# Extra products of constants on TensorE in the half phases without expert blocks

## What is computed

```
x = x + attention(layernorm(x))      # 16 heads of 8; softmax row sums times v, then an output product
x = x + experts(layernorm(x))        # top 2 of 8 experts, 128 -> 512 -> relu -> 128
x = x + selective_scan(layernorm(x)) # 16 states, cumulative sums over tokens
x = x + experts(layernorm(x))        # the same experts again
```

## Time and profile before

| | us |
|---|---|
| median of three runs | 1569.88 (1565.36 to 1571.23) |
| the profiled execution | 1570.4 |
| its span, first to last instruction | 1568.7 |
| PE busy in it | 1017.3 (65%) |
| DVE busy | 827.3 (53%) |
| ACT busy | 743.9 (47%) |
| POOL busy | 629.0 (40%) |
| mean granted clock of TensorE | 0.77 of full speed |

### The profile page before, as it was taken

How to read it: one execution, slowest core, us unless ns; L and a number is a source line. 1 busy time by engine, 2 the same in 40 slices (tenths; PEclk the granted TensorE clock), 3 DMA queues, 4 the chain that set the end, 5 groups by cost and what they waited for, 6 DMA issues and landing times. The chain is left out here.

```text
span 1568.7 us, 18068 instructions
## 1 busy us (share of the span) xinstructions
PE 1017.3 (65%) x5080; PEld 752.7 (48%) x5080; DVE 827.3 (53%) x2789; ACT 743.9 (47%) x2034; POOL 629.0 (40%) x672
## 2 busy tenths in 40 slices
PE   4777689558887673687888643477686536772372
PEld 2554477426664432575576321356375215561272
DVE  4676555555666683556556645254555534545011
ACT  4786666546565662565556513153364232450020
POOL 2101200362424366423223466654444576465303
PEclk8665698678788575888879566788899768896696
DMA  8001244213230012333543111243453222433362
GB/s 255 1 1 34 86 147 136 91 47 95 87 112 16 7 66 83 99 118 92 151 141 95 43 58 57 87 135 118 122 159 122 78 67 91 131 108 97 117 218 73
DMA packets 101812, 150.65 MB, mean 96 GB/s; under 512 B 9840, under 2 KB 72688, under 8 KB 101584
## 3 DMA queue, kind: packets, MB, share of 16 engines
q1 hardware_dynamic: 88832, 129.20, 26.2%
q0 software_dynamic: 8528, 18.19, 4.0%
q10 hardware_dynamic: 4352, 2.10, 0.5%
HBM read 125.39 MB, written 28.25 MB: 98 GB/s over the span
## 5 line engine op out<-in xcount | busy, mean ns | idle before, releaser
L1291 PE MATMUL eo_bank<-wring,hid 128*128 128x128 f32 x1472 | 224.5, 302 | 94.2 <-DVE eos L1015 89.4
L1276 PE MATMUL h_bank<-xT,wring 128*128 128x128 f32 x1472 | 230.0, 306 | 47.5 <-DVE xT L1003 34.4
L1291 PEld LDWEIGHTS eo_bank<-wring,hid 128*128 128x128 f32 x1472 | 204.6, 215 | 106.0 <-issue 66.8
L635 ACT ACTIVATE sc_bank<-sc_bank,nmx 128x256 f32<-128x256 f32 x512 | 229.8, 457 | 51.0 <-DVE nmx L827 36.5
L1276 PEld LDWEIGHTS h_bank<-xT,wring 128*128 128x128 f32 x1472 | 208.9, 216 | 82.5 <-DVE xT L1003 43.7
L508 POOL TENSOR_TENSOR rings<-Rs,Abc 128x512 f32<-128x512 f32 x128 | 162.5, 1290 | 176.3 <-ACT Rs L663 108.5
L709 ACT ACTIVATE hid<-h_bank 128x512 f32<-128x512 f32 x184 | 109.3, 595 | 243.7 <-PE h_bank L1276 221.2
L827 DVE TENSOR_REDUCE nmx<-sc_bank 128x2 f32<-128x512 f32 x256 | 169.8, 685 | 68.5 <-PE sc_bank L1169 51.0
L575 POOL DMA_INDIRECT gbuf<-yg,pos x128 | 122.9, 960 | 180.5 <-issue 106.6
L1225 PE MATMUL sc_bank<-Pw,upto 128*128 128x512 f32 x256 | 164.1, 743 | 44.8 <-DVE Pw L883 43.8
L893 DVE SCALAR_TENSOR_TENSOR rings<-sc_bank,bc,rings 128x128 f32<-128x128 f32 x512 | 142.9, 342 | 80.4 <-PE sc_bank L1225 80.3
(11 more groups left out here) (155 smaller groups left out, 1377.3 us busy)
## 6 DMA issues: line engine op xcount, KB each, us to landing
wring<-wcat SPq DMA_DIRECT2D x184, 512.0 KB
stage<-xg SPq DMA_DIRECT2D x40, 256.0 KB
yg<-eos SPq DMA_DIRECT2D x40, 256.0 KB
wcat<-in_w SPq DMA_DIRECT2D x16, 256.0 KB, 5.4
X<-in_x SPq DMA_DIRECT2D x16, 128.0 KB, 5.8
xg<-xnb,pos POOLq DMA_INDIRECT x128
gbuf<-yg,pos POOLq DMA_INDIRECT x128
out<-X ACTq DMA_DIRECT2D x16, 128.0 KB
```

The costliest lines, as they stand in the source:

```text
L635: last = act.activation(sc[r % NSC][:, c * L:(c + 1) * L], sc[r % NSC][:, c * L:(c + 1) * L], ACT.Exp, bias=nmx[:, c, r:r + 1], accum_out= ...
L1276: last = pe.matmul(hb[b % 2][:, f], wring[:, n % WR, 0, f], xT[:, b % 2], start=True, stop=True)
L1291: last = pe.matmul(eo[:, o:o + P], hid[:, b % 2, f], wring[:, n % WR, 1, f], start=(k == 0), stop=(k == FC - 1))
```

## The change

`keep_warm` is called by PE at the start of each half phase (one product) and behind `run_half` in it (two products), except in the last phase. Where a run is under way it does nothing. Elsewhere it issues products of `ones` and `upto`, 128x128 in float32, into the first 128 columns of the bank `eo`. Nobody reads them, and they signal nobody. Since the bank is that of the runs' results, the products wait, from the first run's end on, for DVE's last copy out of the bank in the run before (event `eo5`).

```diff
+            def keep_warm(n, half, times):
+
+                k = n * HALVES + half
+                spans = [(p * HALVES + h, p * HALVES + h + halves) for p, h, halves in (RUN_FIRST[run] for run in RUNS)]
+                if any(first <= k < last for first, last in spans):
+                    return
+                over = sum(last <= k for first, last in spans)
+                if over:
+                    pe.wait_ge(*run_dve.at(f"eo{STORES - 1}", over - 1))
+                for _ in range(times):
+                    pe.matmul(eo[:, 0:P], ones[:], upto[:], start=True, stop=True)
+
             def phase(n):
                 a, at, c, ct = (m.get(n) for m in (head, tail_a, front, tail_s))
                 o = AT_LATE if a is not None else 0
                 for half in range(HALVES):
+                    if n < PHASES - 1:
+                        keep_warm(n, half, 1)
                     if half == 0 and a is not None:
                         attn_xnT(n, a)
...
                     run_half(n, half)
+                    if n < PHASES - 1:
+                        keep_warm(n, half, 2)
                     if half < 3 and ct is not None:
                         scan_sums(n, ct, 5 + half)
```

## The result

The changed kernel takes 1585.53 us (median of four runs, 1582.71 to 1588.82), the kernel before 1567.62 us beside it (1563.23 to 1571.23). The ratio is 1.0116, 95% interval 1.0079 to 1.0154: slower by over 0.5%, and above the range. The profiled execution took 1587.47 us, its span is 1585.7 us.

The account below looks back on a forecast made before the run. ACT was taken to bound the attention rounds, PE the first few us of a phase. Terms 1, 2, 3, 4, 5: -3.5 - 5.0 - 1.7 + 4.5 + 1.7 = -4.0 us against 1570.4, giving 1566 us, range 1551 to 1580.

Parts of the forecast that it names:

- The price of one product: On PE one product takes 0.22 us at the full clock or 0.43 at the low, a block of three 0.67 or 1.28.
- PE then has no idle time at all: In attention rounds at the low clock PE gets 2.4 us of work where ACT wants 1.2, so the clock rises.
- Phases 0 to 5, 14, 15 and 16 run at 2.4 GHz nearly throughout: With the products, PE's clock stays at the high level almost all through these nine phases.
- a rival about moved waits: Waits of 6.58 and 9.16 us that no instruction ends may go or come: 1557 or 1575 us, chance 0.20.
- Term 1: Phases 1 to 5: the first exponential comes 0.7 us sooner, -0.7 us per phase, -3.5 for five.
- Term 2: Front chains without a run: -2.3 us in phase 15, -1.9 in 23, -0.8 in 9, nothing in 24 and 29; -5.0 together.
- Term 3: Chain at the last scan's end: 2.5 us less, 0.8 of blocks again, -1.7 us.
- Term 4: Phases 14 and 16: PE already back to back at the full clock, four blocks on the path, +4.5 us for both.
- Term 5: Added wait on `eo5` holds up PE's queue: +0.7 us in phase 19, +1.0 in phase 31, +1.7 in all.
- the one I gave 0.02: The clock does not rise; phases 0 to 5 each grow by up to 14 us, 1650 us in all, chance 0.02.
- blocks as the bound at the high clock: PE falls behind in rounds of phases 0 to 5, 14, 16: 2.2 us each, 1586 us, 1578 at half; chance 0.15.
- Full payback: In the four longest stretches without a run, low-clock time gives back half: 159 us, 1411 us, chance 1 in 50.

Follow-up runs that it names:

- the four parts above: Four kernels with the changed kernel's products only in phase 5, phases 0 to 4, phases 8 to 16, or from 19 on: 1.0055, 0.9985, 1.0104, 1.0019.
- rows24: The changed kernel with products only in phases 0 to 4, each over 24 rows instead of 128: 1.0376 of the kernel before.
- waits_only: The changed kernel with the added waits on `eo5` but without any product: 0.9994 of the kernel before.
- h_bank: The changed kernel with all products written to the hidden layer's bank, which needs no wait on `eo5`: 1.0107 of the kernel before.
- not_behind: The changed kernel without the 99 products behind three stalls, in phases 5, 8 and 16 and just after: 1.0041 of the kernel before.
- not_behind_again: The kernel of not_behind run again, beside the changed kernel on one chip: 1.0026 of the kernel before.
- phases19_35: The changed kernel with products only from phase 19 on: 1.0019 of the kernel before.
- changed_again: The changed kernel itself run again, on another chip: 1.0090 of the kernel before.
- phases1_4: The changed kernel with products in phases 1 to 4 alone, none in phase 0: 1.0024 of the kernel before.

## Why the prediction was wrong

It said 1566 us, range 1551 to 1580, and slower with a chance of 0.22. Step by step:

- **The price of one product** was right: 0.67 us for a block at the high clock (100.64 - 99.97 above) and 1.28 at the low one (from 157.97 us, where a block starts in phase 5, to the group at 159.25). The records of a block behind a score are longer, 0.94 and 1.65.
- **"PE then has no idle time at all", so the clock rises.** This step failed. It took the clock's rise in the earlier trace rows, behind two groups of queries and keys over 128 rows, as the answer to a busy PE, and carried it over to rounds in which scores over 24 rows take turns with the blocks. Behind the stall of phase 5 PE was busy with hardly a pause (21.69 of 22.00 us) and the clock stayed at 0.5, where a block and a score cost 2.3 us (175.92 to 178.22 above) and PE, not ACT, set the pace. The cost that the prediction had at nothing there is 9.6 us in phase 5, and the four parts above put most of the rest in phases 8, 9 and 16. The trace of before already held a warning: eight scores in 3.43 us without a pause between them, at the low clock, and no rise. The Trainium skill ("TensorE: Matmul & The Clock Gate", Part 1) lets the clock follow how busy PE has been; of products over few rows it says nothing. The trace of rows24 does not agree with busy time alone: 38.44 of 38.60 us, at the durations of the low level.
- **"Phases 0 to 5, 14, 15 and 16 run at 2.4 GHz nearly throughout"** was right for 0 to 4 and 15 but for a few us, and wrong for 5 and the second half of 16. Phases 8 and 9 were not in it; only the chain of 9 had a term. I read the phases as alike, though phase 5 has the scatter of the first run beside it and the earlier trace rows showed its wait of 6.58 us. I gave that row to a rival about moved waits, not to the clock.
- **Term 1** (-3.5 for phases 1 to 5): phases 1 to 4 gave +0.5 together, inside the ends that stood there. In phase 3 the first exponential came 0.67 us sooner, as laid out, but the rounds, which had no more than 0.06 us for a block, took 0.9 us more. Phase 5 gave +9.6. Phase 0, which had no term, cost 2 us: with the products PE was busy for 24.90 of 25.50 us.
- **Term 2** (-5.0, of it -2.3 in phase 15). From `v_b` to the first `rings` it was 545.10 - 531.68 = 13.4 us before, and 11.8 now: -1.6. The mechanism was right there, and a third smaller. The two rows of after, PE's and POOL's timeline:

```profile
543.68 0.41 PE L1110 MATMUL prep_bank<-ident,v_b 128*128 128x128 f32 x2 [0.32 <-DVE v_b L838]
```

```profile
555.49 6.36 POOL L508 TENSOR_TENSOR rings<-Rs,Abc 128x512 f32<-128x512 f32 x5 [7.28 <-ACT Rs L663]
```

- The gap of 3.10 us ahead of it is 0.32 now: the products hide in it, as forecast. In phase 23, for which -1.9 was forecast, it did not work. The chain from `u_s` to `scan_R`, before and now:

```profile
920.50:932.00 11.50, 5.80 (x19) 3.65 (x19) 4.30 (x17) 2.40 (x8) 8.75 (x10) 0.50 0.08 20
934.90:947.00 12.10, 10.76 (x43) 9.00 (x44) 4.25 (x18) 2.56 (x8) 9.22 (x10) 0.50 0.08 22
```

- PE waits for `u_s` for 7.33 us, no product stands in that wait, the chain begins at the low clock and stays there, and the blocks make it 0.7 us longer (11.45 us before, 12.14 now).
- **Term 3** (-1.7 for the last scan's end): from `y_s` to the first count it was 1433.84 - 1425.58 = 8.3 us, and is 1451.89 - 1444.69 = 7.2: -1.1.
- **Term 4** (+4.5 for the starts of 14 and 16): the start of phase 16, up to the transposition of `y_s`, took 12.2 us and takes 14.4, +2.1 as forecast; in phase 14 it was +0.5. Here too the clock was as I had it:

```profile
577.40:585.70 8.30, 8.30 (x38) 5.46 (x37) 4.37 (x15) 2.42 (x5) 3.49 (x4) 1.00 0.00 0
```

- **Term 5** (+1.7 for the waits on `eo5`): waits_only and h_bank give nothing that can be told from zero. In phase 19 PE does wait, for 2.17 us, as the earlier trace rows had it:

```profile
760.42 0.94 PE L1317 MATMUL eo_bank<-upto,ones 128*128 128x128 f32 x6 [2.17 <-DVE eos L1015]
```

- **The rivals.** What happened is nearest to the one I gave 0.02, that the clock does not rise, but at a few places instead of in six phases, 10 us at the first and not 14 in each. The time is near 1586 us, the figure of another rival (blocks as the bound at the high clock), and that is chance: that rival put 2.2 us on each of eight phases, and phase 3 shows 0.9 in the rounds, made up for at its start. Full payback fell: 181 us of low clock went, and the kernel is 18 us slower. What came back is seen in the stretch of phases 6 and 7 (about 5 us), at the start of a phase and in the chain of phase 15. Else a low clock was mostly beside ACT's work, and where it was not, the blocks took what it gave.

What stays open: no run tells how much of phase 16 is the blocks' doing and how much the long wait's. About a third of the loss (not_behind at 1.0041, not_behind_again at 1.0026) is tied to no single place. The 2 us of phase 0 and what phases19_35 shows are of that size together, but small against the intervals. The wait of ACT in phase 5 that no instruction ends is in the traces of two chips and of the first pair, and not in those of two others; I don't know what it is. No version beat the kernel before.

## What to carry to other kernels

Products that only hold the clock up can hide in idle time while it is up, and cost double from the moment it falls (0.67 and 1.28 us for three); so look for every wait on PE's path in the stretch first, and for what fills PE behind it. Ask then what was late while the clock was low: here little was, since ScalarE led the rounds, and no version with filler could be told faster than the one without. A mean over several like phases hides the one that has a stall.

## What the runs showed of the hardware

- The granted clock did not follow PE's busy share alone. With three products over 24 rows per half phase it was low for 190 us (rows24; PE busy for 38.44 of 38.60 us in phase 2); with three over 128 rows it was high with 25.11 of 26.00 (phase 3 of the changed kernel).
- The same mix of work ran at either level: with a block of three products over 128 rows between scores it stayed high in phases 2 to 4, and did not come back in the 16 us (changed_again) and 27 us (after) behind a wait in phase 5. Groups and blocks over 128 rows at a phase's start came before its rise (phases1_4, phase 1).
- It fell in a wait of PE of 2.85 us (changed_again), and beside one of 1.74 us (after, at 296.39 us), where it stayed high in h_bank without that wait.
- A trace may hold no record of the clock before its first change. The view then shows 1.00 at durations of the low level (rows24, 2.07 us for a group); durations are the surer reading.
